# Perceiver cross-attention, Mamba and quantised FFN on one core: raw dt formed by TensorE in two PSUM banks in place of eight VectorE steps

## The chip, the cores and the metric

One NeuronCore of a Trainium2 chip runs the whole program; nothing is exchanged with other cores. The metric is the device time in microseconds, as the median of several runs. Each engine (TensorE or PE, VectorE or DVE, ScalarE or ACT, GpSimd or POOL, and SyncE or SP, which only issues DMAs) works through its own list of instructions in order, and the lists are tied together by semaphores.

## The reference

The reference computes three residual layers over x, which is 64 batches of 32 rows by 512.

1. Cross-attention with 16 heads of depth 32 over 257 context rows per batch.
2. A Mamba block with 1024 channels and 16 states. With `xz = norm(x) @ in_proj_w`, a causal convolution of four taps and silu give `x_`. Then:

```python
bcd = x_ @ x_proj_w                      # 16 columns of B, 16 of C, and one of dt
dt = softplus(bcd[..., -1:] * dt_w + dt_b)   # one number per row times a weight per channel
dA = exp(dt[..., None] * A);  dBx = (dt * x_)[..., None] * B
h = dA_t * h + dBx_t;  y_t = sum_n h * C     # scan over the 32 positions
out = ((y + x_ * D) * silu(z)) @ out_proj_w
```

3. An FFN of 2048 with activations quantised to 8 bits by a maximum over the whole tensor.

The change touches the argument of softplus alone: for every channel p and row q it is `dt_w[p] * dtraw[q] + dt_b[p]`.

## The kernel before, in words

The 2048 rows are 16 tiles of 128 rows (four batches). Attention and Mamba are software-pipelined over tiles: `schedule` runs `interval(ta, tm, to)` for each tile, in which attention works on tile `ta`, Mamba begins tile `tm = ta - 1` and finishes tile `to = ta - 2`. Tiles 3 to 14 are a hardware loop; the intervals 0 to 2 and 15 are written out, and `tail` finishes the last Mamba tile. An interval has four steps, b = 0 to 3, one for each batch. `schedule` is a list in one order that every engine goes through, and each engine issues only what its own class implements, so the order of the calls is the order on each engine. The scan work of VectorE is spread over the places named "a", "m", "n", ..., "e" by the tables FINISH, BEGIN and their ..._DECAYS.

All of Mamba's channel tensors lie with the channel in the partition, as 8 chunks (IC) of 128 channels by 128 rows. In step b = 1 of an interval, raw dt and softplus go through these calls:

- `mamba_bcd` (PE L1126, ACT L1393): the 33 rows of B, C and dt.
- `dt_row` (PE L1134, ACT L1399): a product with a column of the identity spreads the dt row over all 128 partitions of bank 7, and ACT copies it to `BC[:, 32, :]`.
- `mamba_steps` (DVE L1764): eight tensor_scalar instructions, each multiplying the spread row by the channel's dt_w and adding its dt_b (columns 1 and 2 of `chan`), write `dt`. They stand behind the reciprocal of softmax (L1710) and ahead of the scan work at "n".
- `mamba_softplus` (ACT L1415, L1417, L1420): Abs of `dt`, Exp, and Ln in two halves, behind `normalise` (L1336) and the second `keys_copy` (L1278).
- `mamba_dt` (DVE L1770): max(dt, 0) plus the logarithm, in two halves. `mamba_u` (L1782) and `decays` (ACT L1443) follow.

PE in step b = 1 issues: the second half of the context transposes (L958), the spread row (L1134), `kv_keys` in two halves j = 0 and j = 1 (L992, banks 6 and 7), the gate half of in_proj (`mamba_gate`, L1099), the transposes of the probabilities (L1034), values (L1003), `weigh_values` (L1045, bank 4), `mamba_out` (L1140, bank 5), values again, and then, in step b = 2, the transposes (L958) and `scores` (L1025, banks 2 to 5), which VectorE reads in L1697. In step b = 0 VectorE adds the residual (`x1_write`, L1724) and takes layernorm statistics; POOL and ACT finish the norm, and PE transposes it (L1092) for in_proj.

A float32 product appears in the trace as two instructions: the 16 products of `kv_keys` are 32 records.

In the tail, `mamba_steps(LAST)` stands between `rows_load(LAST, 0)` and `mamba_softplus(LAST)`, ahead of the scan of tile 14's last chunk. The setup (`rest_of_setup`) loads `conv_b`, `dt_w`, `dt_b` and `Dskip` into the four columns of `chan` with one DMA each (L893), on SP's queue ahead of the large weights and of the third batch's context rows.

Of the kernel before, what the change touches and what calls it, by code (L numbers as in the profile page):

```python
# [6 lines left out]
P = 128  # L7
# [13 lines left out]
NT = B // BT  # L21
# [18 lines left out]
def perceiver_kernel(nc, x, ctx_kv, mask, Wq, bq, Wk, bk, Wv, bv, Wo, bo, Win, conv_w, conv_b, Wx,  # L40
# [13 lines left out]
    with ExitStack() as ctx:  # L54
# [35 lines left out]
        chan = sb("chan", [P, 4, IC])  # L90
# [167 lines left out]
        bc_loaded = [sem("b_loaded"), sem("c_loaded")]  # L258
        dt_step = sem("dt_step")
# [89 lines left out]
        def tail(part):  # L349
# [31 lines left out]
            part.mamba_steps(LAST)  # L381
# [55 lines left out]
        def schedule(part, engine):  # L437
# [22 lines left out]
            def interval(ta, tm, to, more):  # L460

                here, front, back = ta is not None, tm is not None, to is not None
                for b in range(BT):
# [127 lines left out]
                    if here:  # L591
                        part.weigh_values(g, ta, b)
# [38 lines left out]
        class Part:  # L631
# [33 lines left out]
            def weigh_values(self, g, t, b): pass  # L665
# [17 lines left out]
            def mamba_steps(self, t): pass  # L683
# [70 lines left out]
        BQKV_DMAS, EARLY_DMAS, OTHER_DMAS = 9, 2, 9  # L754
# [3 lines left out]
        def _(sp):  # L758
# [173 lines left out]
        def _(pe):  # L932
# [10 lines left out]
            class Products(Part):  # L943
# [25 lines left out]
                def kv_keys(self, g, b, ta, tm, to, more):  # L969
# [5 lines left out]
                    for j in range(2):  # L975
                        if b == 0 and j == 0 and to is not None:
# [159 lines left out]

                def mamba_out(self, t):
# [10 lines left out]
                def weights_transpose(self, pieces):  # L1148
                    for n in pieces:
                        pe.wait_ge(wq_loaded[n // FC], 16)  # L1150
                        if n >= 3:
# [90 lines left out]
        def _(act):  # L1242
            act.wait_ge(setup_pool, 2)

            class Functions(Part):
# [92 lines left out]
                def weigh_values(self, g, t, b):  # L1338
# [21 lines left out]
                def mamba_pad(self, t, q):  # L1360

                    if q == 0:
                        wait(act, dt_step, 10 * t)
# [31 lines left out]
                def dt_row(self, t, keys):  # L1395
                    act.wait_ge(dtrow_psum, t + 1)

                    wait(act, dt_step, 10 * t)
                    act.copy(BC[:, 2 * NS, :], bank[7][:, 0:P]).then_inc(dtrow_copied, 1)  # L1399
# [11 lines left out]

                def mamba_softplus(self, t):
# [636 lines left out]
```

## Time and profile before

| what | value |
|---|---|
| median of 3 runs (lowest, highest) | 2023.56 us (2022.76, 2023.82) |
| the profiled execution: its own time, its span | 2018.77 us, 2017.0 us |
| busy in the span: PE, DVE, ACT, POOL | 1853.5, 1851.5, 1622.9, 493.6 us |
| granted TensorE clock, mean | 0.979 |
| the eight steps L1764, all 128 of them | 33.9 us |
| first and last instance of L1764 | 154.0 and 1794.2 us |

The span is the time from the first to the last instruction of the profiled execution; its own time is that run's value of the metric. A busy share over the whole span says little here, since the setup, the 15 intervals and the FFN have different limits. So one interval is read by itself: which engine has no gap in it, and where two engines' streams meet.

### The profile page before, as it was taken

How to read it: one execution, taken by the hardware profiler on the slowest of the kernel's cores; microseconds unless marked ns; L12 is line 12 of the kernel's file. 1: busy time of each engine (PE TensorE's matmuls, PEld its weight loads, DVE VectorE, ACT ScalarE, POOL GpSimd, SP SyncE). 2: the span in 40 equal slices, each digit the busy share in tenths (PEclk: the TensorE clock that was granted, in tenths of full speed). 3: DMA queues.
4: the chain of work that ended last, by engine and by line, in shares of the span. 5: the costliest groups of instructions: out<-in, count | busy, mean ns of one | idle time of the engine just before them, and what ended most of it. 6: DMA issues, size and time to landing. Idle time of an engine off the chain costs nothing. (4 is left out here: it accounts for less than half of the span.)

```text
span 2017.0 us, 43545 instructions
## 1 busy us (share of the span) xinstructions
PE 1853.5 (92%) x14733; PEld 1275.4 (63%) x14748; DVE 1851.5 (92%) x2320; ACT 1622.9 (80%) x4425; POOL 493.6 (24%) x392
## 2 busy tenths in 40 slices
PE   7998998999999999999999999999998999567899
PEld 5576666756575766666676767666666657366444
DVE  1647999999999999999999999999999999999788
ACT  3458888898988889898889788888988888867483
POOL 1001214131414232241413141422314131201013
PEclk9999999999999999999999999999999999789899
DMA  9623333333433333343333334343333333420214
GB/s 300 218 77 95 85 95 85 93 80 85 86 105 74 97 80 75 93 94 90 82 95 80 86 74 115 66 93 87 77 95 85 93 79 91 94 85 11 74 45 143
DMA packets 93456, 189.54 MB, mean 94 GB/s; under 512 B 18768, under 2 KB 39904, under 8 KB 88160
## 3 DMA queue, kind: packets, MB, share of 16 engines
q1 hardware_dynamic: 78448, 133.32, 21.0%
q0 software_dynamic: 14832, 54.01, 14.5%
q8 instruction: 94, 1.54, 0.3%
q14 instruction: 82, 0.67, 0.1%
HBM read 116.12 MB, written 17.18 MB: 66 GB/s over the span
## 5 line engine op out<-in xcount | busy, mean ns | idle before, releaser
L1443 ACT ACTIVATE dA<-dt,A_sb 128x124 f32<-128x124 f32 x2048 | 618.0, 397 | 12.5 <-DVE dt L1770 12.4
L1820 DVE TENSOR_TENSOR_SCAN hb<-dA,hb 128x2048 f32<-128x2048 f32 x118 | 522.4, 4427 | 8.1 <-ACT dA L1443 4.3
L992 PE MATMUL bank<-ctxT,wk_sb 128*128 128x256 f32 x2048 | 466.5, 384 | 30.4 <-ACT Q L1329 19.6
L1003 PE MATMUL bank<-wv_sb,ctxT 128*128 128x512 f32 x1024 | 476.7, 607 | 2.3 <-ACT ctxT L1262 2.3
L992 PEld LDWEIGHTS bank<-ctxT,wk_sb 128*128 128x128 f32 x2048 | 382.1, 191 | 99.7 <-ACT Q L1329 25.3
L1003 PEld LDWEIGHTS bank<-wv_sb,ctxT 128*128 128x128 f32 x1024 | 189.0, 193 | 194.9 <-issue 189.5
L1545 POOL DMA_DIRECT2D hb<-hb x103 | 93.5, 908 | 858.9 <-DVE hb L1826 843.6
L1815 DVE TENSOR_TENSOR hb<-u,BC 128x2048 f32<-128x2048 f32 x118 | 270.4, 2291 | 5.7 <-DVE u L1782 2.6
L1826 DVE TENSOR_TENSOR hb<-hb,BC 128x2048 f32<-128x2048 f32 x117 | 268.9, 2298 | 1.5
L1099 PE MATMUL bank<-xn2T,win_sb 128*128 128x128 f32 x2048 | 239.0, 278 | 0.7 <-ACT xn2T L1358 0.7
L1099 PEld LDWEIGHTS bank<-xn2T,win_sb 128*128 128x128 f32 x2048 | 236.4, 195 | 4.2 <-issue 2.2
L1517 POOL TENSOR_SCALAR maskn<-maskb 128x257 f32<-128x257 f32 x64 | 137.6, 2150 | 260.8 <-DVE soft L1697 258.4
L1299 ACT ACTIVATE Pr<-Pr,soft 128x257 f32<-128x257 f32 x256 | 127.4, 506 | 56.7 <-DVE soft L1697 56.7
L1792 DVE TENSOR_TENSOR hb<-hb 128x512 f32<-128x512 f32 (+2 forms) x248 | 149.6, 603 | 5.0 <-DMA hb<-hb 0.5
L1336 ACT ACTIVATE Pr<-Pr,soft 128x256 f32<-128x256 f32 x256 | 109.0, 503 | 23.6 <-DVE soft L1710 23.6
L1278 ACT ACTIVATE KT<-bank,bqkv 128x256 f32<-128x256 f32 x256 | 105.6, 464 | 26.3 <-PE bank L992 26.2
L1262 ACT ACTIVATE ctxT<-bank,lastT 128x256 f32<-128x256 f32 x256 | 102.5, 479 | 27.8 <-PE bank L958 25.6
L1285 ACT COPY V<-bank 128x512 f32<-128x512 f32 x128 | 74.7, 583 | 58.2 <-PE bank L1003 29.1
L1756 DVE SCALAR_TENSOR_TENSOR xs<-xpad,convw,xs 128x128 f32<-128x128 f32 x384 | 103.7, 347 | 14.9 <-ACT xs L1377 14.4
L1140 PE MATMUL bank<-wout_sb,zs 128*128 128x512 f32 x240 | 106.9, 598 | 0.0
L1034 PE MATMUL bank<-idf,Pr 128*128 128x128 f32 x512 | 79.5, 285 | 29.7 <-ACT Pr L1336 26.7
L1697 DVE CUSTOM_DVE_ANT_0 Pr<-bank,maskn 128x257 f32<-128x257 f32 x256 | 93.1, 421 | 10.8 <-PE bank L1025 10.8
(167 smaller groups left out, 2434.0 us busy)
## 6 DMA issues: line engine op xcount, KB each, us to landing
hb<-hb POOLq DMA_DIRECT2D x103, 512.0 KB, 5.2
ctx_sb<-in_ctx_dram SPq DMA_DIRECT2D x64, 512.0 KB, 4.0
BC<-bcd_dram SPq DMA_DIRECT2D x32, 1024.0 KB, 7.2
maskb<-in_mask_Bx1x1xS_fk_dram SPq DMA_DIRECT2D x64, 128.5 KB, 3.3
wstage<-in_L_ffn_w_dram SPq DMA_DIRECT2D x4, 2048.0 KB, 11.3
x_sb<-in_x_dram SPq DMA_DIRECT2D x16, 256.0 KB, 3.7
win_sb<-in_L_attn_in_proj_w_dram SPq DMA_DIRECT2D x1, 4096.0 KB, 25.1
bo_sb<-bias_dram SPq DMA_DIRECT2D x64, 64.0 KB, 2.0
```

Source lines behind the costliest of these rows:

```text
L992: last = pe.matmul(bank[6 + j][:, (m % 2) * KF:(m % 2 + 1) * KF], wk_sb[:, c, m * P:(m + 1) * P], ctxT[:, c, :], start=(c == 0), stop=(c = ...
L1003: last = pe.matmul(bank[h][:], ctxT[:, c, h * P:(h + 1) * P], wv_sb[:, c, :], start=(c == 0), stop=(c == DC - 1))
L1099: last = pe.matmul(bank[6 + q % 2][:, e * P:(e + 1) * P], win_sb[:, c, n:n + P], xn2T[:, c, :], start=(c == 0), stop=(c == DC - 1))
L1140: last = pe.matmul(bank[5][:], zs[:, c, :], wout_sb[:, c, :], start=(c == 0), stop=(c == IC - 1))
L1299: act.activation(Pr[:, m, :], Pr[:, m, :], ACT.Exp, scale=-1.0, bias=soft[:, 0, m:m + 1], accum_out=soft[:, 1, m:m + 1]).then_inc(exp_done, 1)
L1336: act.mul(Pr[:, m, 0:KF], Pr[:, m, 0:KF], soft[:, 2, m:m + 1]).then_inc(p_ready, 1)
L1443: last = act.activation(dA[:, c % 2, n * BT:(n + 1) * BT, 1:], dt[:, c, :].rearrange("p (b s) -> p b s", s=S)[:, :, 1:], ACT.Exp, scale=A_ ...
L1517: pool.tensor_scalar(maskn[:], maskb[:], -NEG, 1.0, ALU.mult, ALU.mult).then_inc(mask_scaled, 1)
L1792: dve.tensor_tensor(tile[:, 0:n, :], tile[:, 0:n, :], tile[:, n:2 * n, :], ALU.add).then_inc(sum_step, 1)
L1815: ins = dve.tensor_tensor(tile, u[:, c, :].unsqueeze(1).broadcast_to([P, NS, P]), BC[:, 0:NS, :], ALU.mult)
L1820: ins = dve.tensor_tensor_scan(flat, dA[:, c % 2].rearrange("p n s -> p (n s)"), flat, 0.0, ALU.mult, ALU.add)
L1826: ins = dve.tensor_tensor(tile, tile, BC[:, NS:2 * NS, :], ALU.mult)
```

## The change

Raw dt becomes an outer product. The setup puts dt_w and dt_b as rows into `dt_rows`: channels 0 to 511 at partitions 0 and 1, channels 512 to 1023 at partitions 32 and 33, by four DMAs of one row; `chan` keeps two columns, loaded by two DMAs. One small VectorE reduction over the identity makes two columns of `consts`, which are 1 at the partitions 0, 32, ... and at 1, 33, ..., and 0 elsewhere. ACT's copy of the spread dt row becomes an Identity activation with these as scale and bias, so that the row holds dt at partitions 0, 32, ..., ones at partitions 1, 33, ... PE multiplies in `dt_product`: eight products with two rows of contraction, 128 by 128, alternating between row groups 0 and 32, into banks 4 and 5. In an interval this stands between the two halves of `kv_keys` of step b = 1; in the tail behind the sum of chunk 6. ACT's Abs reads the two banks, and Abs and Exp (`mamba_magnitude`) move ahead of `normalise`; the logarithms stay. VectorE's `mamba_dt` reads the banks. `weigh_values` of step b = 1 waits for it (`dt_step`) before it writes bank 4, and so do the later transposes of weights in the tail.

```diff
-        chan = sb("chan", [P, 4, IC])
+        chan = sb("chan", [P, 2, IC])
+        dt_rows = sb("dt_rows", [P, DC, P])
...
             part.rows_load(LAST, 0)
-            part.mamba_steps(LAST)
+            part.dt_product(LAST)
+            part.mamba_magnitude(LAST)
             part.mamba_softplus(LAST)
...
                         part.rows_load(tm, 0)
-                        part.mamba_steps(tm)
...
                     if following and b == 0:
                         part.kv_values(g + 1, 0, range(0, 2))
+                    if b == 1 and front:
+                        part.mamba_magnitude(tm)
                     if here:
                         part.normalise(g)
...
-                    for i, v in enumerate((conv_b, dt_w, dt_b, Dskip)):
+                    for i, v in enumerate((conv_b, Dskip)):
                         sp.dma_start(chan[:, i, :], v.rearrange("(c p) -> p c", p=P)).then_inc(w_loaded, 16)
+                    for r in range(2):
+                        for i, v in enumerate((dt_w, dt_b)):
+                            row = r * DEPTH + i
+                            sp.dma_start(dt_rows[row:row + 1, :, :], v[r * D:(r + 1) * D].rearrange("(o k p) -> o k p", o=1, p=P)
+                                         ).then_inc(w_loaded, 16)
...
                     for j in range(2):
+                        if b == 1 and j == 1 and tm is not None:
+                            pe.wait_ge(scored, DC * g)
+                            self.dt_product(tm)
...
-                def weigh_values(self, g, t, b):
+                def weigh_values(self, g, t, b, tm):
...
+                    if b == 1 and tm is not None:
+                        pe.wait_ge(dt_step, 2 * (tm + 1))
...
+                def dt_product(self, t):
+                    pe.wait_ge(dtrow_copied, t + 1)
+                    if isinstance(t, int) and t == LAST:
+                        pe.wait_ge(wT_copied, 9)
+                    for k in range(DC):
+                        for r in range(2):
+                            rows = slice(r * DEPTH, r * DEPTH + 2)
+                            last = pe.matmul(bank[4 + r][:, k * P:(k + 1) * P], dt_rows[rows, k, :], BC[rows, 2 * NS, :],
+                                             start=True, stop=True)
+                    last.then_inc(dt_psum, 1)
...
-                    act.copy(BC[:, 2 * NS, :], bank[7][:, 0:P]).then_inc(dtrow_copied, 1)
+                    wait(act, dt_psum, t)
...
+                    act.activation(BC[:, 2 * NS, :], bank[7][:, 0:P], ACT.Identity, scale=consts[:, 1:2],
+                                   bias=consts[:, 2:3]).then_inc(dtrow_copied, 1)
...
-                    act.wait_ge(dt_step, 10 * t + 8)
-                    act.activation(soft_tmp, dt[:], ACT.Abs).then_inc(dt_act, 1)
+                def mamba_magnitude(self, t):
+                    act.wait_ge(dt_psum, t + 1)
+                    for i in range(2):
+                        part = soft_tmp[:, DC * i:DC * (i + 1), :].rearrange("p c q -> p (c q)")
+                        last = act.activation(part, bank[4 + i][:], ACT.Abs)
+                    last.then_inc(dt_act, 1)
...
+            dve.wait_ge(ident_loaded, 16)
+            dve.tensor_reduce(consts[:, 1:3], idf[:].rearrange("p (r q) -> p q r", q=DEPTH)[:, 0:2, :], AX.X, ALU.add
+                              ).then_inc(setup_own, 1)
...
-                def mamba_steps(self, t):
-                    dve.wait_ge(dtrow_copied, t + 1)
-                    wait(dve, dA_ready, IC * t)
-                    for c in range(IC):
-                        dve.tensor_scalar(dt[:, c, :], BC[:, 2 * NS, :], chan[:, 1, c:c + 1], chan[:, 2, c:c + 1],
-                                          ALU.mult, ALU.add).then_inc(dt_step, 1)
...
-                        dve.scalar_tensor_tensor(dt[:, half, :], dt[:, half, :], 0.0, soft_tmp[:, half, :],
-                                                 ALU.max, ALU.add).then_inc(dt_step, 1)
+                        dve.scalar_tensor_tensor(dt[:, half, :], bank[4 + i][:].rearrange("p (c q) -> p c q", q=P), 0.0,
+                                                 soft_tmp[:, half, :], ALU.max, ALU.add).then_inc(dt_step, 1)
```

## Rows read from the trace of the kernel before

**Rows 1.** Busy by stretch: start:end, length; PE, PEld, DVE, ACT, POOL; clock, DMA, GB/s

```profile
919.73:1029.36 109.63, 104.93 (x856) 72.42 (x855) 107.32 (x136) 94.95 (x269) 31.00 (x24) 0.98 0.36 87
```

**Rows 2.** Timeline of DVE, one interval: start, length, line, tiles, count [idle before]

```profile
919.73 2.12 DVE L1764 TENSOR_SCALAR dt<-BC,chan 128x128 f32<-128x128 f32 x8
921.76 2.29 DVE L1826 TENSOR_TENSOR hb<-hb,BC 128x2048 f32<-128x2048 f32 x1
...
925.35 1.28 DVE L1770 SCALAR_TENSOR_TENSOR dt<-dt,xpad 128x512 f32<-128x512 f32 x2
...
942.51 0.68 DVE L1906 CUSTOM_DVE_ANT_0 x<-bank,x 128x512 f32<-128x512 f32 x1
...
946.40 0.42 DVE L1697 CUSTOM_DVE_ANT_0 Pr<-bank,maskn 128x257 f32<-128x257 f32 x1
...
996.42 0.67 DVE L1724 TENSOR_TENSOR x<-bank,xbo 128x512 f32<-128x512 f32 x1
```

**Rows 3.** Timeline of PE in the same interval

```profile
920.55 7.31 PE L1099 MATMUL bank<-xn2T,win_sb 128*128 128x128 f32 x64
...
932.79 7.13 PE L1140 MATMUL bank<-wout_sb,zs 128*128 128x512 f32 x16
...
943.73 0.72 PE L1025 MATMUL bank<-KT,Q 32*32 32x257 f32 x32
944.38 0.66 PE L958 MATMUL bank<-idf,ctx_sb 128*128 128x128 f32 x4
944.87 7.14 PE L992 MATMUL bank<-ctxT,wk_sb 128*128 128x256 f32 x32
953.13 2.44 PE L1034 MATMUL bank<-idf,Pr 128*128 128x128 f32 x8 [1.12 <-ACT Pr L1336]
...
1004.29 0.63 PE L1092 MATMUL bank<-idf,ln_out 128*128 128x128 f32 x4 [1.72 <-ACT ln_out L1304]
```

**Rows 4.** Timeline of ACT in the same interval, around softplus

```profile
917.36 0.84 ACT L1278 ACTIVATE KT<-bank,bqkv 128x256 f32<-128x256 f32 x2 [0.66 <-PE bank L992]
919.85 1.71 ACT L1336 ACTIVATE Pr<-Pr,soft 128x256 f32<-128x256 f32 x4 [1.65 <-DVE soft L1710]
...
922.18 1.04 ACT L1415 ACTIVATE xpad<-dt 128x1024 f32<-128x1024 f32 x1
...
924.34 1.15 ACT L1420 ACTIVATE xpad<-xpad 128x512 f32<-128x512 f32 x2
```

**Rows 5.** Timelines of PE and DVE in interval 0, where DVE waits for scores

```profile
76.14 0.71 PE L1025 MATMUL bank<-KT,Q 32*32 32x257 f32 x32
...
77.15 0.43 DVE L1697 CUSTOM_DVE_ANT_0 Pr<-bank,maskn 128x257 f32<-128x257 f32 x1 [4.32 <-PE bank L1025]
```

**Rows 6.** Group by line, weight loads of the scores: count | busy us, mean ns | idle before

```profile
L1025 PEld LDWEIGHTS bank<-KT,Q 32*32 32x32 f32 x2048 | 15.2, 103 | 22.4 <-issue 22.4
```

**Rows 7.** Timelines of DVE and PE in the tail

```profile
1792.39 2.15 DVE L1764 TENSOR_SCALAR dt<-BC,chan 128x128 f32<-128x128 f32 x8 [1.63 <-ACT BC L1399]
...
1800.56 1.28 DVE L1770 SCALAR_TENSOR_TENSOR dt<-dt,xpad 128x512 f32<-128x512 f32 x2
...
1791.99 3.84 PE L1175 MATMUL bank<-hb,idf 128*128 128x128 f32 x32
```

**Rows 8.** Timelines of SP's issues and of PE in the setup

```profile
17.94 0.43 SPq L889 DMA_DIRECT2D idb<-in_ident_b_dram  x1
...
19.66 2.05 SPq L893 DMA_DIRECT2D chan<-in_L_attn_dt_w_dram  x1
21.75 0.58 SPq L893 DMA_DIRECT2D chan<-in_L_attn_dt_b_dram  x1
...
58.34 0.66 PE L958 MATMUL bank<-idf,ctx_sb 128*128 128x128 f32 x4 [3.24 <-DMA ctx_sb<-in_ctx_dram]
```

**Rows 9.** Timelines of ACT and DVE in interval 1, around softplus

```profile
158.15 0.84 ACT L1278 ACTIVATE KT<-bank,bqkv 128x256 f32<-128x256 f32 x2 [1.03 <-PE bank L992]
...
161.72 1.29 DVE L1770 SCALAR_TENSOR_TENSOR dt<-dt,xpad 128x512 f32<-128x512 f32 x2 [5.65 <-ACT xpad L1420]
```

More of the change, by code:

```diff
@@ L258, in perceiver_kernel @@
         bc_loaded = [sem("b_loaded"), sem("c_loaded")]
+        dt_psum = sem("dt_psum")
         dt_step = sem("dt_step")
@@ L591, in interval @@
                     if here:
-                        part.weigh_values(g, ta, b)
+                        part.weigh_values(g, ta, b, tm)
                     if b == 0 and here and not front:
@@ L664, in transpose_p, with weigh_values @@
             def transpose_p(self, g): pass
-            def weigh_values(self, g, t, b): pass
+            def weigh_values(self, g, t, b, tm): pass
             def wo_product(self, t, keys): pass
@@ L682, in dt_row, with dt_product, mamba_magnitude @@
             def dt_row(self, t, keys): pass
-            def mamba_steps(self, t): pass
+            def dt_product(self, t): pass
+            def mamba_magnitude(self, t): pass
             def mamba_softplus(self, t): pass
@@ L752, in apart @@
             engine.sem_inc(passed, 1)
-        BQKV_DMAS, EARLY_DMAS, OTHER_DMAS = 9, 2, 9
+        BQKV_DMAS, EARLY_DMAS, OTHER_DMAS = 9, 2, 11
         @block.sync
@@ L1150, in weights_transpose @@
                         pe.wait_ge(wq_loaded[n // FC], 16)
+                        if n >= 10:
+                            pe.wait_ge(dt_step, 2 * NT)
                         if n >= 3:
@@ L1336, in normalise, with weigh_values @@
                         act.mul(Pr[:, m, 0:KF], Pr[:, m, 0:KF], soft[:, 2, m:m + 1]).then_inc(p_ready, 1)
-                def weigh_values(self, g, t, b):
+                def weigh_values(self, g, t, b, tm):
                     act.wait_ge(o_psum, g + 1)
@@ L1362, in mamba_pad @@
                     if q == 0:
-                        wait(act, dt_step, 10 * t)
+                        wait(act, dt_step, 2 * t)
                     act.wait_ge(in_psum, 4 * t + q + 1)
@@ L1396, in dt_row @@
                     act.wait_ge(dtrow_psum, t + 1)
-                    wait(act, dt_step, 10 * t)
-                    act.copy(BC[:, 2 * NS, :], bank[7][:, 0:P]).then_inc(dtrow_copied, 1)
+                    wait(act, dt_psum, t)
+                    if isinstance(t, int) and t == 0:
+                        act.wait_ge(setup_own, 3)
+                    act.activation(BC[:, 2 * NS, :], bank[7][:, 0:P], ACT.Identity, scale=consts[:, 1:2],
+                                   bias=consts[:, 2:3]).then_inc(dtrow_copied, 1)
                 def gate_silu(self, t):
@@ L1551, in mamba_pad @@
                         return
-                    wait(pool, dt_step, 10 * t)
+                    wait(pool, dt_step, 2 * t)
                     apart(pool)
@@ L1756, in mamba_conv, with mamba_dt @@
                                 dve.scalar_tensor_tensor(acc, src, tap, acc, ALU.mult, ALU.add).then_inc(conv_done, 1)
-                def mamba_steps(self, t):
-                    dve.wait_ge(dtrow_copied, t + 1)
+                def mamba_dt(self, t):
                     wait(dve, dA_ready, IC * t)
-                    for c in range(IC):
-                        dve.tensor_scalar(dt[:, c, :], BC[:, 2 * NS, :], chan[:, 1, c:c + 1], chan[:, 2, c:c + 1],
-                                          ALU.mult, ALU.add).then_inc(dt_step, 1)
-                def mamba_dt(self, t):
-                    for i, half in enumerate((slice(0, IC // 2), slice(IC // 2, IC))):
+                    for i in range(2):
+                        half = slice(DC * i, DC * (i + 1))
                         dve.wait_ge(dt_act, 4 * t + 3 + i)
-                        dve.scalar_tensor_tensor(dt[:, half, :], dt[:, half, :], 0.0, soft_tmp[:, half, :],
-                                                 ALU.max, ALU.add).then_inc(dt_step, 1)
+                        dve.scalar_tensor_tensor(dt[:, half, :], bank[4 + i][:].rearrange("p (c q) -> p c q", q=P), 0.0,
+                                                 soft_tmp[:, half, :], ALU.max, ALU.add).then_inc(dt_step, 1)
                 def mamba_u(self, t):
```

10 lines of the change are left out of this document (5 added, 5 removed).

## The prediction, made before the changed kernel ran

> **What bounds the kernel now.** I first read the busy times of single intervals. The interval shown runs from one L1764 to the next: 109.6 us, with VectorE busy for 107.3 of them; the 2.3 left are the small gaps between its 136 instructions. TensorE is busy for 104.9, ScalarE for 95.0 [rows 1]. So VectorE is the limit, and TensorE has only about 5 us of air. Next I read VectorE's timeline over this period, which starts with L1764 at 919.73: it shows no idle time worth naming, so each step waits for the one before it on the engine [rows 2]. Then TensorE's timeline, to find where its air is. In this interval it idles 1.12 us at 953.13 (for ACT's probabilities) and 1.72 us at 1004.29 (for the normed rows of x1, which hang on VectorE's L1724 at 996.42 through POOL and ACT); between such a 1004.29 of one interval and the 953.13 of the next it has no stop [rows 3]. That unbroken stretch ends, for VectorE, at the scores of step b = 2: PE L1025 at 943.73, DVE L1697 at 946.40 [rows 2, 3]. The new products are put into exactly this stretch. How close are the two there? Where VectorE really waits for scores, it starts 77.15 − 76.14 = 1.01 us after PE's L1025 starts [rows 5]. At 943.73 it could therefore have begun at 944.74; it began at 946.40, so TensorE is ahead by 1.66 us. This number decides the case.
>
> **VectorE, removed.** The eight steps take 921.76 − 919.73 = 2.03 us of its stream per interval [rows 2]. `mamba_dt` reads a PSUM bank in place of `dt`. Its instruction takes 0.68 us per half now, and L1724, which has the same 128x512 with one operand in PSUM, takes 0.67 [rows 2]; I count the swap at nothing (ends −0.1 and +0.1 us for the pair).
>
> **TensorE, added.** Eight products of 128 columns. The gate product is 32 products of that size in 7.31 us, 0.228 each [rows 3], so one after the other they are 1.83 us. But they alternate between two groups of rows and write two banks. No row shows 32-row by 128-column tiles; the nearest is L1025, 16 products of 257 columns in 32 by 32 tiles. It lasts 944.38 − 943.73 = 0.65 us, while one full-array product of 256 columns lasts 7.14/16 = 0.446 [rows 3]. So the small tiles, four groups of rows among them with a bank each, run almost entirely side by side, and switching into them and out costs about 0.20 us. Their 32 weight loads, of 103 ns each, go into the same 0.65 us, so these overlap too [rows 6]. With pairs side by side: 4 × 0.228 + 0.20 = 1.1 us. With no overlap: 1.83 + 0.20 = 2.0 us, and, if every change of row group also exposes something, 2.3 (half the 0.20 for every further pair). The low end is 0.2 us, if the products slip into the gaps of the key products. I take x = 1.1, the row that it is nearest to being L1025, and keep 0.2 and 2.3 as ends.
>
> The row in the trace shows small tiles side by side. The Trainium skill, "TensorEngine Tiling (Array Packing)", section "Key Properties", says that tiles execute loads and products in parallel but that changing the tiling mode drains the engine; the 0.20 us above would be that drain. The Trainium skill, "TensorE: Matmul & The Clock Gate", section "LDWEIGHTS (loading the stationary operand)", prices a load by its columns, at P/1.2 ns; my estimate by it for 16 loads of 128 columns, if they queue behind each other, is 1.7 us. By that the total would be near 2024, the second rival below. That speaks against the change; what the same page says about loads in another row group (they overlap) speaks for the forecast.
>
> The added waits on TensorE: the row for the products is ready long before (ACT copies it right after the context, and `kv_keys` j = 1 waited for that same copy already); `scored` of the running batch is due before as well. `weigh_values` waits for VectorE's `mamba_dt`, which ends at 926.6 now, and TensorE gets there about 932, just ahead of L1140 at 932.79 [rows 2, 3]: 5 us of cover, cost nothing; if it went, `mamba_out` and the scores would queue behind.
>
> **ScalarE, moved.** Abs and Exp go ahead of `normalise`. ACT idles 0.66 us before the key copy at 917.36 and 1.65 us before `normalise` at 919.85 [rows 4], so Abs falls into a gap. The first key copy starts when half j = 0 is done, so the products start near 917.2 and end near 918.4 with their latency. Abs 918.4 to 919.5, Exp to 920.6 (1.04 each by [rows 4]), `normalise` 1.6 to 922.2, key copy 0.7 to 922.9, first logarithm (half of 1.15) ready at 923.6. VectorE now wants it at 925.35 − 2.03 = 923.3. It waits about 0.35 us, and dt is there 1.7 us earlier than before. Second key copy and probabilities come 0.7 us later than now; TensorE needs them behind 3.7 us of gate product, so that is hidden. The copy with a scale and a bias may take 0.1 to 0.2 us more, and lies ahead of ACT's 0.66 us of idle time: nothing.
>
> **The sum of an interval.** VectorE would gain 2.03 − 0.35 = 1.68 by its own stream. But the scores of b = 2 arrive x later, with a lead of only 1.66: it can gain no more than 1.66 − x = 0.56 us. The stall does not add to the ACT wait, it swallows it. From there to L1724 of the next interval VectorE is alone (50.0 us, 946.40 to 996.42 [rows 2]), and TensorE's 1.12 us at 953.13 takes up the delay. `mamba_out` ends at 939.92 and L1906 starts at 942.51 [rows 2, 3]: with x and 1.7 us earlier the two just meet, ahead of the scores. So 0.56 us per interval, for the 14 intervals 2 to 15: 7.8 us.
>
> **Interval 1.** VectorE idles 5.65 us before L1770 and waits for ACT: its logarithms stand behind the second key copy at 158.15 [rows 9]. Abs and Exp (2.1 us) go ahead of it, while the key products and copy come x later: about 0.7 us gained.
>
> **Tail.** The steps wait for the row (1.63 us) and take 2.1 us; L1770 follows at 1800.56 [rows 7]. After the change the scan of chunk 7 starts without them, but the products stand behind the 3.84 us of chunk sums from 1791.99 [rows 7]: done near 1797, Abs, Exp and logarithm (1.1, 1.1, 0.6) near 1800.1. Gain 0.3 us; ends −0.7 and 2.
>
> **Setup.** Two DMAs of 4-byte elements with 2.63 us of issue go [rows 8], four single rows come, at about 0.45 us each (the identity's one-piece DMA takes 0.43 [rows 8]). That is 0.8 us on SP's queue, ahead of the big weights and of the context rows for which TensorE idles 3.24 us at 58.34 [rows 8]; TensorE runs on from there almost without a stop, so it counts. The rows are also cheaper for the DMA engines. I take 1.0; ends 0 and 3. The reduction over the identity falls into VectorE's wait for the first transposes.
>
> **Total.** 7.8 + 0.7 + 0.3 + 1.0 = 9.8 us. The profiled execution took 2018.77 us for its span of 2017.0, so it would take 2009.0. The median of the runs is 4.79 us above it, and I add that: 2013.8 us.
>
> **Rivals.**
>
> *The whole saving (chance 0.13).* The lead of 1.66 us is no bound, because the products cost little (x near 0.2: two rows of contraction slip between key products). Then 2.03 − 0.35 = 1.68 less nothing: 1.46 to 1.68 per interval, 14 × 1.6 = 22.4, with 2.0 elsewhere 24.4 us: 1999.2 us. For it: VectorE is the limit, by every view. Against it: each product of 128 columns costs 0.228 us in the gate product whatever it computes.
>
> *Given back on TensorE (chance 0.27).* The pairs overlap in part or not at all, x = 1.5 to 2.0. Per interval 1.66 − x = 0.16 to −0.34, over 14 intervals +2.2 to −4.8; with 2.0 gained elsewhere −4.2 to +2.8, mostly within 4 us: 2023 us.
>
> *TensorE becomes the limit (chance 0.15).* x = 2.3: eight products one by one and a drain at each change of row group. Each interval then loses 0.64 us at the scores of b = 2, 9.0 in all, less 2.0: 2030.6 us. It ends on this side from x = 1.66 + 2.0/14 = 1.80. The loads of 128 columns speak for it, L1025's overlap against it.
>
> *The change does not do what it says:* that the banks are not read by ACT in the gap, because `normalise` is already waiting. That costs at most 0.7 us of ACT and is inside the numbers above.
>
> **How the numbers follow.** The forecast has 0.45, with its own range 2008 to 2019 (x from 0.8 to 1.5 and the setup from 0 to 3). A run is told from no change beyond 0.2%, 4.05 us. Faster by more: the forecast, the whole saving and the lucky edge of the second rival, 0.61. Slower by more: the third rival less its near edge, 0.12. Within: 0.27. The range that leaves out 2 in 10 is 2000 to 2028.
>
> **What would show it.** Right: L1764 gone; per interval one stall of VectorE at L1697 of step b = 2, 1.0 to 1.5 us, released by PE L1025; a period of about 109.0 us; the 1.12 us before L1034 gone; eight products (16 records) in about 1.1 us from the end of j = 0 to the start of j = 1. Wrong: a period of 108 us without that stall (whole saving), or of 110 us with a stall of 2.5 us (TensorE the limit). The forecast fails if the distance between the halves of `kv_keys` grows by under 0.6 or over 1.5 us, or if VectorE stalls longer at L1770 than at L1697.

## The result, and the profile after

The changed kernel takes 2043.12 us (median of 4 runs, 2040.91 to 2044.04), against 2023.36 us for the kernel before beside it (2022.76 to 2023.82): 1.0102 times the time, 95% interval 1.009 to 1.0114. So it is slower by 19.8 us where 9.8 us less were forecast, and outside the range. The profiled execution has a span of 2039.1 us, 22.1 us more than before.

First, where in the program the time went. The start of the write of x1 (L1724 before, L1765 after) marks each interval, so differences of these starts cut the span into parts. Per part, in us:

| part | forecast | measured |
|---|---|---|
| start to the first write of x1 (121.53, now 125.21) | -1.0 | +3.7 |
| interval 1 (108.09, now 109.38) | -0.7 | +1.3 |
| interval 2, written out (109.03, now 108.90) | -0.6 | -0.1 |
| third to sixteenth write (1426.12, now 1441.89) | 13 x -0.56 = -7.3 | +15.8 |
| sixteenth write to the end (252.23, now 253.72) | -0.3 | +1.5 |

The loss is in the loop. Its turns took 109.6 us before (nearly all); now all but the first (109.2) take 110.0 to 112.0, mostly a shorter and a longer one in turn. VectorE's timeline in one interval, to be laid beside [rows 2], where none of these rows has a wait:

```profile
953.02 0.69 DVE L1941 CUSTOM_DVE_ANT_0 x<-bank,x 128x512 f32<-128x512 f32 x1 [0.95 <-PE bank L1167]
...
957.53 0.43 DVE L1738 CUSTOM_DVE_ANT_0 Pr<-bank,maskn 128x257 f32<-128x257 f32 x1 [0.53 <-PE bank L1038]
...
1007.56 0.67 DVE L1765 TENSOR_TENSOR x<-bank,xbo 128x512 f32<-128x512 f32 x1
...
1009.05 0.43 DVE L1738 CUSTOM_DVE_ANT_0 Pr<-bank,maskn 128x257 f32<-128x257 f32 x1 [0.83 <-issue]
```

The first two waits together are the stall forecast: `out_sum` has to wait for `mamba_out`, which the forecast had just meeting, and the scores of step b = 2 come late, 0.95 + 0.53 = 1.48 us (1.0 to 1.5 forecast, all at the scores). From the scores to the next write of x1 it is 50.03 us, as in [rows 2] (50.02). The third wait has no like before. It has no releaser ("issue"), and it stands at the second counted instruction of the loop's body, right behind the jump back. TensorE's timeline, beside [rows 3]:

```profile
928.71 1.16 PE L1160 MATMUL bank<-BC,dt_rows 2*128 2x128 f32 x16
929.80 3.72 PE L1005 MATMUL bank<-ctxT,wk_sb 128*128 128x256 f32 x16
933.36 7.31 PE L1114 MATMUL bank<-xn2T,win_sb 128*128 128x128 f32 x64
...
945.60 7.13 PE L1167 MATMUL bank<-wout_sb,zs 128*128 128x512 f32 x16
...
956.53 0.72 PE L1038 MATMUL bank<-KT,Q 32*32 32x257 f32 x32
...
1016.36 0.63 PE L1107 MATMUL bank<-idf,ln_out 128*128 128x128 f32 x4 [2.64 <-ACT ln_out L1333]
```

The eight products (16 records) take 929.80 - 928.71 = 1.09 us from start to start. The stop ahead of the normed rows, 1.72 us before, is 2.64 here: the statistics of x1 stand on VectorE behind the third wait.

A view of all waits of an engine, grouped, shows the whole loop at once (columns: line waited for; us in total, times, longest). VectorE from the third to the sixteenth write of x1, changed kernel:

```profile
DVE x L1941 <- PE bank L1167: 12.3, 13, 1.0
DVE Pr L1738 <- issue: 9.9, 11, 1.3
DVE Pr L1738 <- PE bank L1038: 7.0, 13, 0.7
DVE xs L1797 <- ACT xs L1406: 6.0, 7, 0.9
```

and the same stretch of the kernel before, where the costliest wait of all was

```profile
DVE soft L1710 <- ACT Pr L1299: 2.8, 13, 0.7
```

Eleven waits for issue, one behind each jump back of the 12 turns, 9.9 us. Then 6.0 us in seven waits for ScalarE's convolution. Where these come from the granted clock shows. The busy table by stretch (columns as in [rows 1]) has, for the place where the in-projection L1114 runs in the turn at 1007.56:

```profile
1017.30:1020.70 3.40, 3.40 (x19) 3.40 (x17) 3.26 (x2) 3.40 (x11) 0.95 (x2) 0.50 0.90 162
```

The clock is at its lower level, 1.2 GHz (0.50), for 3.4 us. It falls there at 460.9 and 573.6 and from then on in every second interval, some 222 us apart (795.4, 1017.3, 1239.2, 1461.0, 1682.9; the last is interval 15, behind the loop), behind the stop at L1107 that has grown; the in-projection is late by it, then ScalarE's first taps, then VectorE:

```profile
1028.74 1.51 DVE L1797 SCALAR_TENSOR_TENSOR xs<-xpad,convw,xs 128x128 f32<-128x128 f32 x4 [0.86 <-ACT xs L1406]
```

The length of the stop alone doesn't decide it: 3.01 us in the turn at 1118.61 is followed by no fall, 2.27 us in the turn at 452.73 is. Why it is every second one stays open. The kernel before had six such stretches in its loop too, one of them in this critical place (at 1114.9, in the interval of 111.8 us).

Last the table of DMA queues, cut to the same stretch (packets, MB, share). Kernel before, and changed kernel:

```profile
q8 instruction: 67, 1.10, 0.3%
q14 instruction: 64, 0.52, 0.1%
```

```profile
q8 instruction: 113, 1.85, 0.5%
q14 instruction: 119, 0.97, 0.2%
```

These queues carry the engines' own instructions. q14 went from 5 packets of 8 KB a turn to 10. In the window 1007.0 to 1008.3, at the jump back, the queue has one packet:

```profile
q14 instruction: 1, 0.01, 2.8%
```

This gave the theory for the experiments. **Theory:** the changed kernel has another number of VectorE instructions ahead of the loop and in it (126 counted ones a turn in place of 136); by this the loop's body lies otherwise in the code, part of it is fetched again at each turn, and VectorE waits for it at the head. **Rivals:** it is TensorE's code (q8 grew too), or the products themselves, or only the later time at which the loop starts.

### The profile page after: what moved, and what is told of

Same layout as the page of the kernel before. It is cut to its first block and busy times, and to the rows that moved or that the text cites. A ratio compares the mean times of both kernels' runs of the same rounds, so it can differ in the third digit from the quotient of the medians.

```text
span 2039.1 us, 43896 instructions
## 1 busy us (share of the span) xinstructions
PE 1876.9 (92%) x14989; PEld 1297.8 (64%) x15004; DVE 1825.7 (90%) x2193; ACT 1623.5 (80%) x4441; POOL 496.5 (24%) x392
## 3 DMA queue, kind: packets, MB, share of 16 engines
q8 instruction: 140, 2.29, 0.4%
q14 instruction: 137, 1.12, 0.2%
## 5 line engine op out<-in xcount | busy, mean ns | idle before, releaser
L1016 PE MATMUL bank<-wv_sb,ctxT 128*128 128x512 f32 x1024 | 469.8, 599 | 2.3 <-ACT ctxT L1291 2.3
L1114 PE MATMUL bank<-xn2T,win_sb 128*128 128x128 f32 x2048 | 243.6, 282 | 0.7 <-ACT xn2T L1387 0.7
L1114 PEld LDWEIGHTS bank<-xn2T,win_sb 128*128 128x128 f32 x2048 | 241.9, 198 | 3.4 <-issue 1.3
L1365 ACT ACTIVATE Pr<-Pr,soft 128x256 f32<-128x256 f32 x256 | 108.9, 503 | 1.1 <-DVE soft L1751 1.1
L968 PEld LDWEIGHTS bank<-idf,ctx_sb 128*128 128x128 f32 x512 | 58.2, 144 | 63.1 <-issue 29.7
```

Of the source, the lines that this page charges most:

```text
L1016: last = pe.matmul(bank[h][:], ctxT[:, c, h * P:(h + 1) * P], wv_sb[:, c, :], start=(c == 0), stop=(c == DC - 1))
L1114: last = pe.matmul(bank[6 + q % 2][:, e * P:(e + 1) * P], win_sb[:, c, n:n + P], xn2T[:, c, :], start=(c == 0), stop=(c == DC - 1))
L1365: act.mul(Pr[:, m, 0:KF], Pr[:, m, 0:KF], soft[:, 2, m:m + 1]).then_inc(p_ready, 1)
```

## The experiments

In the table: median and 95% interval of the ratio to the kernel before on the same chip; from the profiled execution, the start of the first write of x1, the 13 intervals from the third to the sixteenth, the waits for issue in them, and the packets of q14 in a usual turn.

| kernel | us | ratio | x1 first | 13 intervals | issue | q14 |
|---|---|---|---|---|---|---|
| before | 2023.36 | | 121.53 | 1426.1 | 0 | 5 |
| changed | 2043.12 | 1.009 to 1.0114 | 125.21 | 1441.9 | 9.9 | 10 |
| e1_pad_dve | 2021.00 | 0.9992 to 1.0011 | 125.64 | 1421.1 | 0 | 5 |
| e2_pad_pe | 2057.05 | 1.0155 to 1.0189 | 141.36 | 1443.3 | 12.0 | 10 |
| e3_no_product | 2020.93 | 0.998 to 1.0 | 125.16 | 1425.6 | 11.5 | 10 |
| e4_before_pad | 2039.02 | 1.0065 to 1.0099 | 124.78 | 1442.4 | 8.1 | 10 |
| e5_rows_late | 2019.37 | 0.9987 to 1.001 | 123.94 | 1421.1 | 0 | 5 |
| e6_pad_no_product | 2003.76 | 0.9896 to 0.9925 | 123.74 | 1405.4 | 0 | 5 |
| e7_pad_75 | 2022.68 | 0.999 to 1.0008 | 121.54 | 1424.0 | 0 | 5 |
| e8_pad_115 | 2022.10 | 0.9994 to 1.0014 | 125.04 | 1423.0 | 0 | 10 |
| e9_scores_first | 2015.80 | 0.9958 to 0.9981 | 125.72 | 1417.1 | 0 | 5 |
| e10_sum_later | 2020.06 | 0.9983 to 1.0008 | 125.37 | 1424.4 | 0 | 5 |
| e11_before_order | 2031.73 | 1.0033 to 1.0059 | 124.63 | 1432.1 | 0 | 5 |
| e12_values_split | 2014.34 | 0.9963 to 0.9984 | 123.49 | 1415.9 | 0 | 5 |

The kernel before was measured again beside each group of experiments (medians 2021.1 to 2022.4 us), and the ratios go by these. The columns from the profiled execution are of a single one, which took 4.2 us more than the median in e8 and e9 and 7.1 us more in e10, so small differences in them carry little.

**Where VectorE's code lies (e1).** Nothing of the work is changed; a counter that nobody waits for is raised 15 times ahead of the loop.

```
             dve.memset(xmax[:, 0:1], LOWEST).then_inc(setup_own, 1)
             dve.wait_ge(ident_loaded, 16)
+            for _ in range(15):
+                dve.sem_inc(passed, 1)
```

> The changed kernel with 15 empty VectorE instructions (semaphore increments) ahead of the tile loop, so that the loop's code starts where it stood in the kernel before. Theory (the wait of 0.5 to 1.3 us that VectorE shows behind the first instruction of every loop turn, released by nothing but its own issue, is code being fetched, and depends on where the loop's code lies): the 11 waits go, about 10 us come back, and with them part of the half-clock stretches: near 2030 us. Rival (the wait is a real one on another engine that the profile does not show, or TensorE's code is what is late): unchanged, 2043 us.

It took 2021.0 us, 22.1 less than the changed kernel, where some 13 less were expected. Up to the third write of x1 VectorE has 468 instructions on record in the kernel before, 453 in the changed kernel and 468 again here. The waits of VectorE in the 13 intervals are now only the forecast ones, to the tenth those of the changed kernel:

```profile
DVE x L1943 <- PE bank L1167: 12.3, 13, 1.0
DVE Pr L1740 <- PE bank L1038: 7.0, 13, 0.7
```

No wait for issue is left and no stretch of low clock ahead of 1737.5, where the kernel before has one too (1736.1). Eleven of the 13 intervals take 109.2 to 109.5 us, the other two 108.7 and 109.7. So the place of VectorE's code cost the changed kernel 20.8 us in these intervals (1441.9 - 1421.1). 9.9 are the waits at the head, 6.0 those behind the low clock; 4.9 are left over, of which the trace shows 0.6 in each turn with a low-clock stretch and 1.7 in the last interval, without a releaser of their own. The last interval is in doubt: its stretch of low clock comes in e7 and e8 (below) as well, without any wait at the head, and by these two the place is worth 17.9 and 18.9 us.

**TensorE's code (e2), and the products (e3).** e2 puts 188 such counts at TensorE's start; e3 issues the products only in the first Mamba tile (the later ones compute with the banks' old contents).

```
+            for _ in range(188):
+                pe.sem_inc(passed, 1)
             pe.wait_ge(ident_loaded, 16)
```

```
-                    for k in range(DC):
...
-                    last.then_inc(dt_psum, 1)
+                    if isinstance(t, int) and t == 0:
+                        for k in range(DC):
...
+                        last.then_inc(dt_psum, 1)
+                    else:
+                        pe.sem_inc(dt_psum, 1)
```

> The changed kernel with 188 empty TensorE instructions in the setup, which moves TensorE's loop code by a multiple of a code block against the kernel before. If the code fetch of TensorE causes the loss, the time falls towards 2030 us; if it is VectorE's, it stays at 2043 us (plus or minus 2 for the setup).

> The changed kernel with the eight products only in the first Mamba tile; in all later tiles TensorE only signals, and ACT and VectorE work on what lies in the two banks. It leaves out the outer product of 15 tiles. Theory (the chain of TensorE from the normed rows to the scores of b = 2 bounds the interval, 1.1 us of it are the products): VectorE's stalls of 0.95 and 0.5 us in b = 2 go, and each interval is 1.1 us shorter: 2043 - 16 = 2027 us, less if the half-clock stretches change. Rival (the loss is at the loop head alone): under 5 us.

Both keep the waits at the head, 12.0 and 11.5 us, and the 10 packets. e2 lost 16 us more in the setup, not the 2 expected: TensorE's first instruction came at 29.66 us in place of 4.72. Neither TensorE's code nor the products make the waits, nor does a later start, for e2's loop starts 16 us later with the same waits. e3 gained 22.2 us over the changed kernel, where 16 were expected, and far more than the rival allowed: without products the stalls at `out_sum` (L1941 of the changed kernel) go, a first hint that the products hold the period.

**The kernel before, moved (e4).** The same fault, put into the kernel before by 113 counts at VectorE's start:

```
             dve.memset(xmax[:, 0:1], LOWEST).then_inc(setup_own, 1)
+            for _ in range(113):
+                dve.sem_inc(passed, 1)
```

> The kernel before with 113 empty VectorE instructions in the setup, which puts the start of its loop code at the same place within an 8 KB block as in the changed kernel. Theory (place of the code): waits at the loop head appear and the time rises by some 10 us, to 2034. Rival (the place does not matter, the length or another engine does): 2023.5 to 2026 us.

2039.0 us, 0.65 to 0.99% slower (2034 expected), with the waits at the head:

```profile
DVE Pr L1699 <- issue: 8.1, 11, 1.1
DVE xs L1758 <- ACT xs L1377: 6.0, 7, 0.9
```

Its 581 instructions up to the third write of x1 are the 453 of the changed kernel and 128. Most of the changed kernel's loss can be given to the kernel before without touching what it computes. The counts themselves cost at most 3.3 us, up to the first write of x1. On the queue that grew in the changed kernel, q8, there are fewer packets here than in the kernel before (67), and e1 has the changed kernel's 113 and no waits, so the waits don't go with q8:

```profile
q8 instruction: 58, 0.95, 0.3%
```

**More places (e7, e8).** The first fence's edit with 75 and with 115 counts, to try a rule: that the code comes in blocks of 128 instructions (8 KB), and that the waits come when the loop's body of some 290 instructions touches four of them and not three.

> The changed kernel with 75 increments on VectorE in place of 15. Theory (the loop's body of code is fetched in blocks of 128 instructions, and it matters only how many blocks the body of some 290 instructions touches): 15 and 75 both lie in the same stretch of 90 or so places where it touches three, so the loop's head shows no wait in this kernel either, the instruction queue carries 5 packets a turn, and the total is that of 15 with 60 more increments in the setup, 2021 to 2024. Rival (it is the number of instructions in all, or the exact alignment of the loop's start, that counts): the waits at the loop's head are back, 0.5 to 1.3 us a turn, 10 packets a turn, total about 2043.

> The changed kernel with 115 increments on VectorE. Theory of the blocks of 128 instructions: the changed kernel without increments has its loop straddle a fourth block, and 115 increments bring it back near that place, so that the waits at the loop's head return (0.5 to 1.3 us a turn, 10 packets a turn) and the total is 2040 to 2047. Rival (any addition ahead of the loop helps, for example by a longer setup or because the loop was too near the program's start): no waits, 5 packets a turn, total 2021 to 2026.

e7 is as the rule says. e8 missed: waits and 2040 to 2047 us were expected. It splits the rule in two. The packets are back,

```profile
q14 instruction: 119, 0.97, 0.2%
```

as many as in the changed kernel, but VectorE never waits and the time is that of e1 (2022.1 us). So the five packets more cost nothing by themselves here. That they cost only where the code is needed right behind the jump back is my reading, made after the run. By the rule 115 = 128 - 13 counts put the edge of a block 13 instructions further into the body than in the changed kernel, where VectorE waits two instructions in. The rule's constants were fitted to the kernels run before, it foretold the packets of e7 and e8, and where the blocks lie was not measured. What is shown is that the place of the loop in VectorE's code makes the waits; that they are waits for a fetch is inferred from the packets.

The Trainium skill, "Runtime: NRT & Kernel Launch", section "Instruction fetch mechanics", says that a taken branch whose target is outside the window of code at hand forces a fetch by DMA before the engine can go on. The changed kernel agrees with it, with 0.46 to 1.29 us a turn, but e8, with the same packets, shows no such wait; where it says that blocks are 16 KiB, the packets here are of that size on q8 (1.85 MB in 113) but of half of it on q14.

**The setup (e5).** e1, with the four row DMAs of L902 issued behind the mask of the third group, in `load_context(2)`, where they are no longer ahead of the weights:

```
                     sp.dma_start(maskb[:], mask_rows[g].partition_broadcast(P)).then_inc(mask_loaded, 16)
+                    if isinstance(g, int) and g == 2:
+                        with nc.allow_non_contiguous_dma(reason="rows, once"):
+                            for r in range(2):
...
```

> The changed kernel with the 15 increments of a counter on VectorE ahead of the loop (as in the first padded kernel, 2021.0 us) and with the four DMAs of the dt rows issued later on SP, behind the mask of the third group, so that the big weights and the context rows of the setup are no longer behind them. Theory (the setup's loss is these four issues on SP's queue, which push the context rows that TensorE waits for at 59.5): the first L1765-group write of x1 comes near 122 us, as in the kernel before (121.53; 125.64 in the first padded kernel), and the total falls by 3 to 4 us to about 2017.5. Rival (the setup's loss hangs on the half clock of TensorE at 58.2 us, or on the reduction over the identity, not on SP's queue): x1 first stays at 125 to 126 and the total at 2021.

The first write of x1 comes 1.7 us sooner, not the 3.6 expected, and the total of 2019.4 us is not told from e1's by the intervals of the ratios. Three timelines of TensorE at the same stop, changed kernel, e1 and e7:

```profile
59.52 1.11 PE L968 MATMUL bank<-idf,ctx_sb 128*128 128x128 f32 x4 [5.47 <-DMA ctx_sb<-in_ctx_dram]
```

```profile
60.40 1.12 PE L968 MATMUL bank<-idf,ctx_sb 128*128 128x128 f32 x4 [6.38 <-DMA ctx_sb<-in_ctx_dram]
```

```profile
58.37 0.66 PE L968 MATMUL bank<-idf,ctx_sb 128*128 128x128 f32 x4 [1.10 <-DMA ctx_sb<-in_ctx_dram]
```

In the first two the transposes take 1.11 us in place of 0.66: the clock is at its lower level from 58.1 us on, for 6.8 us. It falls when TensorE has stood for 4.1 us of its stop. In e7 VectorE starts 6 us later, TensorE's work ahead of the stop ends later too, the stop is 1.10 us, the clock stays up, and the first write of x1 comes at 121.54, as before the change, though the rows are loaded early. So the four early rows don't by themselves make the loss. SP issues the third batch's context rows at 38.04 us in the kernel before, at 39.49 in the changed one, and at 40.35 in e1 and 38.50 in e7, whose lists on SP are the same. And e11 (below) has the setup of the kernel before, DMA by DMA, yet it issues these rows at 39.05 and stops for 4.55 us:

```profile
59.38 0.66 PE L961 MATMUL bank<-idf,ctx_sb 128*128 128x128 f32 x4 [4.55 <-DMA ctx_sb<-in_ctx_dram]
```

The clock is at its lower level behind that for 3.4 us, and the first write of x1 comes at 124.63. So 3.1 of the 3.7 us come there without the change. The rows differ from one execution to the next by as much as the effect looked for, and how the 3.7 us divide is not settled.

**How much the products hold (e6).** e1 and e3 together.

> The changed kernel with the 15 increments on VectorE and without the eight products on TensorE in every Mamba tile but the first (the banks keep what they held). Theory of the two chains: with the code no longer fetched at the loop's head, and x = 1.28 us taken off TensorE, VectorE is held by itself and by the lead of 1.66 us alone: a period of 107.9 to 108.2 us in place of 109.25, no wait for the scores of step b = 2 on VectorE, total about 2003 to 2006. Rival (something else than the products' time holds the period: the logarithms on ScalarE, or the waits between the steps): a period of 108.8 to 109.3 us, total 2015 to 2021.

2003.8 us, and a turn of 107.97 us, as the theory of the two chains says, but for one thing: it expected no wait for the scores, and 0.4 us a turn is left. Two numbers come out of it. Without products a turn is 109.63 - 107.97 = 1.66 us shorter than before: this is the lead read from [rows 2, 3, 5], and what VectorE still waits for is again the scores:

```profile
DVE Pr L1743 <- PE bank L1038: 5.5, 13, 0.7
```

And the products cost 109.27 - 107.97 = 1.30 us of a usual turn, all of what they add to TensorE.

**Taking the stalls away (e9, e10, e11, e12).** If the scores of step b = 2 are the bound, an order that brings them earlier must pay, and one that only removes the stall at `out_sum` must not. Two edits of the schedule: the first half of the next context's transposes goes behind the scores in step b = 2, and VectorE's product of 2.29 us (L1852 in e1) ahead of the sum of x2.

```
-                    if following and 0 < b < BT - 1:
+                    if following and b == 1:
                         part.kv_turn(g + 1, 0, 0)
...
```

```
                     place("d")
+                    if b == 1:
+                        place("e")
                     if b == 1 and back:
                         part.out_sum(to)
                         part.out_norm(to)
-                    place("e")
+                    if b != 1:
+                        place("e")
```

e9 has both, on top of e5; e10 only the second; e11 both, in the kernel before.

> The changed kernel with the 15 increments on VectorE and the late dt rows (2019.4 us, 109.3 us per turn), and with two changes of order that take VectorE off TensorE's chain at the scores of step b = 2: VectorE's product with the hidden states (2.29 us) goes ahead of the sum of x2, where it waited 0.95 us for the bank of mamba_out; and on TensorE the first half of the transposes of the next context (0.53 to 0.60 us) goes behind the scores of step b = 2 in place of ahead of them, where VectorE waited 0.53 us. Theory (these two stalls, 1.48 us together, are the same 1.28 us of products given back): both go or nearly go, the turn takes 108.0 to 108.4 us as it does with no products, and the total is 2003 to 2009. Rival (TensorE has no air left, 106.2 of the turn being busy, and gives the time back at its next stop, or ScalarE does): the stalls go but others of the same sum come, 109.0 us or more, total 2016 to 2021.

> The same as the kernel with both changes of order, with the first of them alone: VectorE's 2.29 us go ahead of the sum of x2, and TensorE's order stays. Theory (the stall at the sum and that at the scores swallow each other, the scores set the time): the wait of 0.95 us for mamba_out goes, the wait for the scores grows from 0.53 to about 1.5 us, and the turn stays at 109.2 to 109.4 us, total 2018 to 2021. Rival (each stall costs its own time): 108.3 us per turn, total about 2006 to 2009.

> The kernel before with the same two changes of order and nothing else. Theory (there the scores come 1.66 us ahead of VectorE, so making them earlier gives nothing, and the steps stay on VectorE): the turn stays at 109.6 us, total 2021 to 2025. Rival (the order itself is better, whatever the change): a turn of under 109.2 us, total under 2017.

e10 is as forecast: the wait for `mamba_out` is gone, and the one for the scores has taken all of it, in the 13 intervals

```profile
DVE Pr L1745 <- PE bank L1043: 20.7, 13, 1.7
```

(19.3 = 12.3 + 7.0 in e1), with a turn of 109.3 us, but for two of 111.3 and 111.4 with a stretch of low clock. e9 missed its number: 108.8 us a turn and 2015.8 us, not 2003 to 2009, and better than the rival's 109.0. My sum took both stalls away, but the moved transposes give the scores only some 0.4 us (a wait of 1.15 in place of 1.58 in one turn), and the rest stays:

```profile
DVE Pr L1745 <- PE bank L1043: 15.1, 13, 1.3
```

In the kernel before the same order is harmful, 0.33 to 0.59% slower, which neither theory nor rival had. The scores of b = 2 wait there for the sum of x2, which now comes 2.29 us later:

```profile
952.12 0.73 PE L1028 MATMUL bank<-KT,Q 32*32 32x257 f32 x32 [2.29 <-DVE stats L1909]
```

All but two turns take 110.0 us or more, and VectorE now waits for scores there, 0.37 us a turn. I had asked only how early TensorE is, not what the moved step releases. e12 adds to e9 that the last two of the eight value products of step b = 1 go behind the scores.

```
                         part.scores(g, ta, b, to)
+                    if here and b == 2:
+                        part.kv_values(g, 1, range(DC - 1, DC))
...
-                        part.kv_values(g + 1, 1, range(DC))
+                        part.kv_values(g + 1, 1, range(DC - 1 if b == 1 else DC))
```

> The kernel with both changes of order (2015.8 us, 108.8 us per turn, of which VectorE still waits 1.15 us for the scores of step b = 2), with the last two of the eight value products of step b = 1 (0.9 us of TensorE) moved behind those scores. Theory (the way from the normed rows to these scores is TensorE's alone, and 1.15 us of it is all that VectorE still waits for): the wait falls to about 0.25 us, the turn to 107.9 to 108.1 us, the period without any products, total 2003 to 2008. Rival (ScalarE's copy of the values now stands in front of its probabilities and context copies, which come 1.4 us later, and TensorE stops for these as long): the wait at the scores falls all the same, but VectorE or TensorE loses it again within the step, 108.6 us or more, total 2014 to 2020.

The rival had it, 2014.3 us and 108.9 us a turn: the wait for the scores falls to a third, but ScalarE's copy of these values now stands ahead of its context copies, its probabilities and, behind these, its decays. The loss shows in the decays, for which VectorE waits, and hardly on TensorE (stops of 0.29 and 0.15 us in one turn).

```profile
DVE hb L1864 <- ACT dA L1488: 11.1, 13, 0.9
DVE Pr L1747 <- PE bank L1045: 4.8, 13, 0.4
```

e9 and e12 both beat the kernel before, by 0.2 to 0.4%, and the changed one by about 1.3%; between these two the runs don't decide.

## Why the prediction was wrong, step by step

*The lead of 1.66 us.* Right. e6 measures it as 1.66, and the scores bound the turn as said. The stall came in two pieces, since `mamba_out` came too late for its sum as well; e10 shows that the piece at the sum costs nothing by itself.

*VectorE, removed.* Right. The eight steps are gone, and `mamba_dt` takes 1.29 us for its pair from PSUM (e1), 1.28 before.

*TensorE, added, x = 1.1.* A little small. From L1107 to the scores of b = 2 it is 49.06 us before (894.67 of the interval ahead to 943.73) and 50.35 in e1 (898.52 to 948.87): x = 1.29. Of this 1.09 are the products, and 0.20 lie in the key products on both sides, which take 3.65 + 3.56 us from start to start in the changed kernel and 7.01 before. This fits pairs that run side by side, as the row of the scores suggested; no run puts all eight into one row group. The gain of a turn is then 1.66 - 1.29 = 0.37; e1 has 109.63 - 109.27 = 0.36.

*ScalarE, moved.* The wait of 0.35 us at `mamba_dt` did not come: in the 13 intervals VectorE waits for the logarithm once, 1.0 us. TensorE's stop at the probabilities went as forecast, from 1.12 to 0.15 us.

*The sum of an interval.* This is the step that failed. "0.56 us per interval, for the 14 intervals" takes every other cost of a turn as it was, that is, the move of VectorE's code at nothing, without a reason. What the runs show in its place: the edit changes the number of VectorE's instructions, and by it a turn has 0.5 to 1.3 us of waiting at the loop's head and, in every second turn or so, 3.4 us of low clock on the way. 20.8 us by e1, and by e4 16.3 in the kernel before. No rival had it: all three were about the products.

*Interval 1.* Forecast -0.7, came +1.3. The logarithms are earlier, as said, but they were not the last link. VectorE's scan waits for the second decay half, and ScalarE copies the transposed probabilities ahead of it; those stand behind the products on TensorE. ScalarE and VectorE, changed kernel:

```profile
170.66 0.58 ACT L1377 COPY PT<-bank 128x512 f32<-128x512 f32 x1 [2.99 <-PE bank L1047]
...
174.14 4.42 DVE L1855 TENSOR_TENSOR_SCAN hb<-dA,hb 128x2048 f32<-128x2048 f32 x1 [4.80 <-ACT dA L1481]
```

Before:

```profile
165.67 0.59 ACT L1348 COPY PT<-bank 128x512 f32<-128x512 f32 x1 [0.80 <-PE bank L1034]
...
169.16 4.42 DVE L1820 TENSOR_TENSOR_SCAN hb<-dA,hb 128x2048 f32<-128x2048 f32 x1 [2.62 <-ACT dA L1443]
```

From the first write of x1 the copy is at 44.14 before and at 45.45 after: later by 1.31, x again. This was only read from the traces; e3 and e6 keep the products of this one tile.

*Setup.* Forecast -1.0, came +3.7. The two scattered DMAs that went did not take their issue time along: the one left behind them took it over.

```profile
20.48 3.03 SPq L898 DMA_DIRECT2D chan<-in_L_attn_D_dram  x1
23.56 0.49 SPq L902 DMA_DIRECT2D dt_rows<-in_L_attn_dt_w_dram  x1
...
39.49 2.44 SPq L771 DMA_DIRECT2D ctx_sb<-in_ctx_dram  x1
```

The DMA of D had taken 0.58 us before, behind those of dt_w (2.05 us in [rows 8]) and dt_b; now, as the first behind conv_b, it takes 3.03. That it waits there for the queue is argued, not shown. From it to the issue of `wo_sb` it is 24.96 - 20.48 = 4.48 us, where the three scattered DMAs took 23.00 - 19.66 = 3.34: 1.1 us longer, not 0.8 shorter. Of the 1.45 us by which the context rows are issued later, 0.89 are there ahead of all this (an issue at 15.76 in place of 14.87). The low clock came on top, but e11 has most of the loss without the change.

*Tail.* Forecast -0.3, came +1.5, and 1.2 in e1, where the loop is undisturbed. Not tested, and hardly to be told from chance: e1 takes 253.5 us from the sixteenth write to the end and e8, which differs from it by idle counts alone, 257.9. The forecast's own terms add up to 1799.8 and not 1800.1, 0.8 us gained and not 0.3, which changes nothing of this.

Without the place of the code the change is worth nothing that can be measured: 2021.0 us, ratio 0.9992 to 1.0011. The gain in the loop, 5.0 us (1426.1 - 1421.1), is paid back in the profiled executions in setup (+4.1), interval 1 (+1.5) and tail (+1.2).

## What to carry to other kernels

Work moved off a full engine is worth only its lead at the next meeting with the engine that takes it over, less what that engine pays; measure the lead first, and don't add up stalls that swallow each other. In a loop of some hundred instructions on an engine, an edit also moves the code: look for waits with no releaser right behind the jump back and for the packets of the instruction queues, and run one copy padded by a few idle instructions before judging the edit. A stop of TensorE that grows can cost more than itself, by the clock behind it.

## What the runs showed of the hardware

- Where a loop's code lies on VectorE is worth 1% here: 17.9 to 20.8 us of the 13 intervals in the changed kernel (e7, e1), 16.3 in the kernel before (e4), with nothing changed but idle counts ahead of the loop.
- Ten packets a turn on the instruction queue in place of five cost nothing in e8, where VectorE shows no wait behind the jump.
- Eight products of two rows by 128 columns, alternating between two groups of rows and two banks, take 1.09 us, where eight of the gate product's take 1.83; the key products on both sides take 0.20 us longer (7.21 in place of 7.01).
- 188 idle instructions at TensorE's start put off its first work from 4.72 to 29.66 us (e2).
- The same list of setup DMAs on SP reached the third batch's context rows 1.0 us later in e11 than in the kernel before (39.05 in place of 38.04 us), and the first write of x1 moved by 3.1 us.
